# GpSimd's order around its row gathers, one pass for all rotary angles, and the query scaling on ScalarE

## The reference

```python
q = rmsnorm((x @ Wq.T).reshape(B, S, 32, 128), q_norm_w)      # B = 32, S = 32, x is 32 x 32 x 512
k = rmsnorm((x @ Wk.T).reshape(B, S, 8, 128), k_norm_w)
v = (x @ Wv.T).reshape(B, S, 8, 128)
pos = cache_seqlens[:, None] + arange(S)
q, k = rope(q, pos), rope(k, pos)                             # cos and sin of pos / 10000^(2i/128)
k_all = concat([k_cache[block_table], k]); v_all = concat([v_cache[block_table], v])   # 512 + 32 keys
probs = softmax(where(valid, q @ k_all / sqrt(128), -1e30))   # 4 query heads share a key head
x = x + (probs @ v_all) @ Wo.T
```

## Time and profile before

| | |
|---|---|
| median of 3 runs | 1675.08 us (1672.77 to 1676.43) |
| the profiled execution | 1681.27 us, its span 1679.5 us |
| PE busy, share of the span | 1383.3 us, 82% |
| DVE | 998.1 us, 59% |
| POOL | 983.9 us, 59% |
| ACT | 769.5 us, 46% |
| mean granted clock of TensorE | 0.92 |
| DMA | 207.04 MB, 123 GB/s over the span |

### The profile page before, as it was taken

The page is one execution under the profiler, slowest core; times in us unless marked ns, Lnnn a source line. Parts: engine busy times, 40 slices in busy tenths (PEclk is TensorE's granted clock), DMA queues, the critical chain, the costliest instruction groups (busy, mean ns, idle before and its releaser), DMA issues. The chain is left out here.

```text
span 1679.5 us, 29186 instructions
## 1 busy us (share of the span) xinstructions
PE 1383.3 (82%) x8896; PEld 1255.8 (75%) x8896; DVE 998.1 (59%) x2478; ACT 769.5 (46%) x1965; POOL 983.9 (59%) x1264
## 2 busy tenths in 40 slices
PE   3678888897878898887887888898787888888899
PEld 2577778786768787776777777787677887777887
DVE  5755656565565665556655555566666565555664
ACT  3444454444454444445444454444445444445541
POOL 5556666656665556666646666556666555665610
PEclk8799999998899999889998999999989998889999
DMA  5453343345343434435335343333535343433431
GB/s 188 146 156 121 96 129 101 107 126 163 115 148 108 130 107 132 125 91 157 125 115 170 96 125 100 107 115 126 172 116 156 105 118 120 125 96 124 120 103 51
DMA packets 73244, 207.04 MB, mean 123 GB/s; under 512 B 12177, under 2 KB 12465, under 8 KB 73009
## 3 DMA queue, kind: packets, MB, share of 16 engines
q0 software_dynamic: 40960, 134.25, 26.6%
q1 hardware_dynamic: 31392, 69.53, 13.1%
q10 hardware_dynamic: 816, 2.29, 0.4%
HBM read 195.77 MB, written 12.36 MB: 124 GB/s over the span
## 5 line engine op out<-in xcount | busy, mean ns | idle before, releaser
L1062 POOL DMA_INDIRECT kv_rows<-in_kv,step_idx x512 | 510.4, 997 | 188.6 <-issue 132.7
L815 DVE CUSTOM_DVE_ANT_0 soft<-SX,mask 128x544 f32<-128x544 f32 x256 | 185.0, 723 | 342.9 <-PE SX L181 342.4
L397 PE MATMUL KT<-ident,kv_rows 128*128 128x128 f32 x1024 | 177.7, 302 | 241.6 <-DMA kv_rows<-in_kv,step_idx 234.8
L397 PEld LDWEIGHTS KT<-ident,kv_rows 128*128 128x128 f32 x1024 | 128.8, 153 | 259.1 <-issue 236.2
L637 ACT ACTIVATE soft<-soft,min_all 128x544 f32<-128x544 f32 x256 | 191.9, 749 | 260.2 <-DVE min_all L815 257.3
L633 ACT ACTIVATE pT<-PT 128x640 f32<-128x640 f32 x256 | 178.8, 698 | 279.5 <-PE PT L438 279.4
L449 PEld LDWEIGHTS O<-pT,kv_rows 128*128 128x128 f32 x2048 | 283.4, 206 | 17.1 <-ACT pT L633 3.0
L449 PE MATMUL O<-pT,kv_rows 128*128 128x128 f32 x2048 | 290.2, 288 | 1.4 <-ACT pT L633 1.4
L181 PE MATMUL SX<-kT,qT_hi 128*128 128x288 f32 (+1 forms) x1024 | 255.2, 341 | 14.4 <-DVE qT_lo L861 11.7
L615 ACT ACTIVATE kT<-KT 128x512 fp32r<-128x512 f32 x256 | 151.3, 591 | 230.7 <-PE KT L397 230.7
L181 PEld LDWEIGHTS SX<-kT,qT_hi 128*128 128x128 f32 x1024 | 185.3, 219 | 18.7 <-DVE qT_lo L861 13.1
(11 more groups left out here) (207 smaller groups left out, 2604.4 us busy)
## 6 DMA issues: line engine op xcount, KB each, us to landing
mask<-mask_rows SPq DMA_DIRECT2D x64, 272.0 KB, 3.3
stage<-in_wqkv SPq DMA_DIRECT2D x22, 512.0 KB, 5.2
x_raw<-in_xT SPq DMA_DIRECT2D x32, 256.0 KB, 3.9
kv_rows<-in_kv,step_idx POOLq DMA_INDIRECT x512, 3.7
stage<-in_wo SPq DMA_DIRECT2D x16, 512.0 KB, 3.8
y_tile<-y_running SPq DMA_DIRECT2D x32, 256.0 KB, 3.3
y_running<-y_tile SPq DMA_DIRECT2D x31, 256.0 KB, 4.1
out<-kv_rows SPq DMA_DIRECT2D x8, 256.0 KB, 2.0
```

The costliest lines, as they stand in the source:

```text
L397: tr = nc.tensor.transpose(KT[:, c * P:(c + 1) * P], kv_rows[:, b, c, h * D:(h + 1) * D], ident[:, :])
L815: V.tensor_tensor_reduce(scores[:, p % 2, :], SX[:, SX_AT:SX_AT + KEYS], mask[:, b, :], 1.0, BIG, ALU.add, ALU.min, min_all[:, p:p + 1]).t ...
L1062: G.indirect_dma_start(kv_rows[:, b, c, :], None, kv[:, :], bass.IndirectOffsetOnAxis(ap=step_idx[:, b * LC + c:b * LC + c + 1], axis=0)). ...
```

## The change

It has five parts.

- **GpSimd's order.** The gather of b = 3 comes first in a step, with its indices taken in one copy with the others in the step before. Then `rotate_sum` for k = 0, the indices of all four batch elements, gather(0), `rotate_sum` for k = 1, gather(1), `rotate_sum` for k = 2, gather(2), the table.
- **What left GpSimd.** `keep_v` is now four ScalarE copies of 32 rows each (the rest of `v_own` is zeroed once). The mean square is a small VectorE operation (`mean_square`, at pairs 1, 3 and 5). The scaling of the rotated queries by `rstd` is four ScalarE copies of 128x128 with a scale operand (`scale_q`, at pairs 3 and 5, after `exponent`). The keys are still scaled on GpSimd.
- **TensorE.** In pair 7 the first 6 matmuls of `project_out` stand ahead of `score` instead of behind it.
- **The angles.** All 8 tiles in one pass, one range reduction for sine; the cosine is Sin(pi/2 - |angle|), by a scale and a bias of the activation. The tables of the first step are made on VectorE, the row indices on GpSimd.
- **The start.** The blocks of weights are split into high and low parts by halves, the activation table for Exp is loaded before the first block is taken, the mask row is made earlier, and the first pairs' work is put in another order.

The core of the diff (`idx_ready`, `v_zero`, `row_in` and the like are semaphores; the start's new order is left out):

```diff
+            def scale_q(i, h):
+                nth = i * NBLK + h + 2
+                act.wait_ge(sm["sum_ready"], nth)
+                act.wait_ge(sm["pow_ready"], nth)
+                act.wait_ge(sm["q_turned"], i * GK + h)
+                act.nop(nofuse=True)
+                for r in range(REP):
+                    cols = slice(r * D, (r + 1) * D)
+                    scaled = nc.scalar.activation(q_rot[:, cols], rope_u[:, cols], ACT.Copy, scale=rstd[:, r:r + 1])
+                scaled.then_inc(sm["rot_ready"], 1)
+
+            def keep_v(i):
+                act.wait_ge(sm["raw_ready"], i * NBLK + 1)
+                act.wait_ge(sm["pv_done"], CREDIT + i * PAIRS)
+                act.nop(nofuse=True)
+                for b in range(ROWS):
+                    rows = slice(b * SEQ, (b + 1) * SEQ)
+                    kept = nc.scalar.activation(v_own[rows, b, :], v_next[rows, :], ACT.Copy)
+                kept.then_inc(sm["v_own_ready"], 1)
...
+                    if not last and p in (3, 5):
+                        scale_q(i + 1, p // 4)
                     if not last and p == 6:
                         take_qT(i + 1, 1)
...
+                    if not last and p == PAIRS - 1:
+                        keep_v(i + 1)
...
+            def mean_square(i, k):
+                n = GK if k == 0 else REP
+                dve.wait_ge(sm["sq_ready"], i * NBLK + k + 1)
+                V.tensor_scalar(meansq[:, k, 0:n], sumsq[:, k, 0:n], 1.0 / D, EPS, ALU.mult, ALU.add
+                                ).then_inc(sm["ms_ready"], 1)
...
+                    if p == PAIRS - 1:
+                        project_out(i, 0, (0, REP // 2), g * HALVES + WO_FIRST + 2)
                     if p + 2 < PAIRS:
                         score(i, p + 2)
...
-                    if p == PAIRS - 1:
-                        project_out(i, 0, (0, REP // 2), g * HALVES + WO_FIRST + 2)
...
                 G.tensor_tensor(rope_u[:, 0:w], rope_u[:, 0:w], rope_v[:, 0:w], ALU.add).then_inc(sm["sum_ready"], 1)
+                pool.wait_ge(sm["ms_ready"], nth)
+                pool.wait_ge(sm["rot_ready"], nth - 1)
+                G.tensor_tensor(rstd[:, 0:n], meansq[:, k, 0:n], minus_half[:, 0:n], ALU.pow).then_inc(sm["pow_ready"], 1)
                 pool.wait_ge(sm["sum_ready"], nth)
                 pool.wait_ge(sm["pow_ready"], nth)
-                if k == 0:
-                    pool.wait_ge(sm["kT_new_done"], i)
-                    dst = k_rot[:, :]
-                else:
-                    pool.wait_ge(sm["q_turned"], i * GK + k - 1)
-                    dst = q_rot[:, :]
+                if k > 0:
+                    return
+                pool.wait_ge(sm["kT_new_done"], i)
...
-                for k in range(2):
-                    make_rstd(i + 1, k)
-                    rotate_sum(i + 1, k)
-                for row in range(ROWS - 1):
+                b = ROWS - 1
+                pool.wait_ge(sm["pv_done"], CREDIT + i * PAIRS)
+                pool.nop(nofuse=True)
+                gather(b, 0, LC)
+                if last:
+                    return
+                rotate_sum(i + 1, 0)
...
+                for row in range(ROWS):
                     pool.wait_ge(kv_in[row], (i + 1) * 16 * LC)
-                take_indices(tn, 0, ROWS - 1, 2 * i + 3)
+                take_indices(tn, i + 2)
                 next_values(0)
-                make_rstd(i + 1, 2)
+                rotate_sum(i + 1, 1)
+                next_values(1)
                 rotate_sum(i + 1, 2)
+                next_values(2)
                 if not (final and fixed and t == TILES - 2):
                     make_table(i + 2, (t + 2) % TILES if fixed else t + 2)
-                next_values(1)
-                next_values(2)
```

More of the change, by code:

```diff
@@ L121, in program @@
         minus_half = sb("minus_half", [P, REP])
+        half_pi = sb("half_pi", [P, 1])
         row_i = sb("row_i", [BATCH, 1], I32)
@@ L240, in next_tile, with table_parts @@
             return (g + 1, 0) if isinstance(t, int) and t == TILES - 1 else (g, t + 1)
+        def table_parts(t):
+            c, s = ((a[:, t, :] if isinstance(t, int) else a[:, bass.ds(t, 1), :].rearrange("p a n -> p (a n)"))
+                    for a in (cos, sin))
+            for z in range(2):
+                for f in range(2):
+                    cols = slice(f * 64, (f + 1) * 64)
+                    other = slice((1 - f) * 64, (2 - f) * 64)
+                    yield table[:, 2 * z, cols], c, norm_w[:, z, cols]
+                    yield table[:, 2 * z + 1, cols], s, norm_w[:, z, other]
         block = ctx.enter_context(nc.Block())
@@ L381, in proj @@
                         pe.wait_ge(sm["x_ready"], i + 1)
+                    if k == NBLK - 1 and new_keys_first:
+                        pe.wait_ge(sm["kT_new_ready"], i + 1)
                     pe.wait_ge(sm["raw_ready"], i * NBLK + k)
@@ new lines, in _ @@
+            pool.wait_ge(sm["idx_ready"], 1)
+            for j in range(PPC):
+                q = slice(j * PSIZE, (j + 1) * PSIZE)
+                G.tensor_scalar(row_base[q, :], pages_f[q, :].rearrange("p (a j) -> p a j", j=PPC)[:, :, j],
+                                float(PSIZE), in_page[q, 0:1], ALU.mult, ALU.add).then_inc(sm["idx_ready"], 1)
+            pool.wait_ge(sm["idx_ready"], 1 + PPC)
+            take_indices(0, 1)
+            gather(0, 0, LC)
+            G.memset(v_own[:, :, :], 0.0).then_inc(sm["v_zero"], 1)
```

235 lines of the change are left out of this document (97 added, 138 removed).

## The result

The changed kernel took 1500.52 us (median of 4 runs, 1498.61 to 1503.25), against 1673.92 us (4 runs) for the kernel before: a ratio of 0.8969, 95% interval 0.8942 to 0.8997. So it is 10.3% faster. The forecast was 1480 us, 20.5 us or 1.4% too low, and the range held the time. In the experiments all chips were not alike: the kernel before took between 1669 and 1688 us on them. The changed kernel ran on two chips, 1500.5 and 1501.1 us, while the kernel before took 1674 and 1688 on them, so its ratio differs between them (0.8969 and 0.8887). The times of variants of the changed kernel are therefore set against 1500.5 to 1501.1, and differences of a few us are read only between kernels of one chip. Two executions of variants ran slow (1524.8 us with the scaling back on GpSimd, 1852.1 us with the scaling in pair 4), and the times given for these two are medians of the others.

A forecast was written before the change was run, and what follows sets the result against it. TensorE was taken as the bound, waiting 234.8 us for gathered rows behind GpSimd's work. From 1675.1 us, -339 (waits and lower clock) + 155 (given back) - 11.5 (start) gave 1480 us, range 1395 to 1595.

The forecast's parts named there:

- the sum: Whole kernel: 339 us saved in the steps, 155 given back, 11.5 saved at the start, together -195.5 us.
- The start: Ahead of the steps: angles in one early pass and earlier first products bring -11.5 us, bounds 6 and 16.
- The keys: TensorE's waits for gathered rows at pairs 5 and 7 go, 234 us, with the gather starting at 13.6 us.
- The given-back 5.0 us: Pairs 4 to 7, per step: later scaled queries, `pT` and projection cost 1.1, 0.5, 1.9 and 1.5 us.
- The lower clock, 105 us: Pairs 5 and 7: TensorE's lower clock after key waits costs 3.4 us a step over 31 steps, and goes.
- The 16 us that the range allowed for those: Tiles 6, 7 and 0: weight splitting, until now partly under the key wait, may cost about 1 us each.
- my walk through the new order: Ahead of the steps: first product 2 us earlier, queries' transposes 3 to 4, first pair at 48 us.
- Edits at nothing: In the steps: `keep_v`'s ScalarE copies, VectorE's mean squares and GpSimd's lost work were charged no time of their own.
- The clock rival: Pairs 4 to 7: four gaps in 20 us lower the clock, 3.4 us a step stay, 1585 us; chance 0.18.
- The keys were not late: Pair 5: rival with keys 4 to 5 us later, about 2.5 us of waiting left, 1617 us; chance 0.10.
- the 1.06 us at which the gain would have been gone: ScalarE's eight scaling copies a step: slower rival, no gain at 1.06 us each, 1735 us at 1.3; chance 0.05.
- Less given back: Pairs 4 to 7: rival with only ScalarE's load left, about 1.7 us a step, 1378 or halfway 1430; chance 0.20.

The follow-up runs named there:

- the order alone: Kernel before with only GpSimd's step order changed, gathers of b = 0 and 1 ahead of the next block's work: 1459.32 us, on another chip 1472.23.
- the scaling in pair 4: Changed kernel with the first query block's four ScalarE scaling copies moved from pair 3 to behind pair 4's `pT` and `kT` copies: 1468.58 us.
- the projection behind the scores: Changed kernel with the first six output projection matmuls of pair 7 back behind `score`: 1485.90 us.
- the copies run twice: Changed kernel with four more 128x128 scaling copies on ScalarE ahead of the real four in both blocks, into an unread tile: 1576.32 us.
- with both causes taken away: Changed kernel with the first block's scaling copies behind pair 4's copies and pair 7's first six projection matmuls behind `score`: 1471.92 us.
- The angles alone: Kernel before with only the one-pass angles for all eight tiles and the cosine from the sine's argument: 1681.77 us, ratio 0.9963.

## Why the prediction was right, and by how much its steps missed

**Where the 20.5 us are.** From the first pair's start to that of the last step, the 31 steps took 59.48 to 1603.86 before and take 54.36 to 1422.84 now: 1544.4 and 1368.5 us, 175.9 saved where the sum has 339 - 155 = 184. Some 5 of these 8 us are the sum's own: it counts 234 us of waits for all steps, while 31 steps like the one it reads, with 7.37 us of them, hold 228.5. The start gives 5.1 us where it has 11.5. The last step and the end are as before (75.6 us in both). Together 181.1 against 195.5, 14.4 short. The other 6.2 us are the choice to go by the median of before instead of its profiled execution. The changed kernel's profiled execution (span 1498.4) lies at its median, and against 1681.27 us the forecast would have been 1485.8.

**The keys: right.** The gather was put at 13.6 us after the step's start and is at 13.3; 234 us of waits were to go and 228.8 went. The order alone shows that GpSimd's order does all of it. What left GpSimd was not needed for this, and the prediction, which credited the order and let the rest "only make room", was right on that too.

**The given-back 5.0 us: right in sum and nearly so pair by pair.** The step was forecast at 42.8 and is 42.9. Pairs 4 to 7 were put at 5.8, 3.6, 5.2 and 9.9 us (full-clock pairs of 4.7, 3.1, 3.3 and 8.4, plus 1.1, 0.5, 1.9 and 1.5) and take 5.69, 4.02, 5.60 and 9.28. The named mechanisms are there: ScalarE's wait of 2.73 us at pair 3 (forecast 2.9), the copies' 1.28 (1.2), the power's end at 20.6 (20.9), pair 5's wait for the earlier output (0.41 us, `oT_lo` ready at 26.4, forecast 26.6), the second mean square, power and copies (29.3, 30.4 and 31.8, forecast 28.7, 29.8 and 31.1), and `project_out`'s wait for `oT_lo` in pair 7. The first is shown by the scaling in pair 4, the last by the projection behind the scores, and the load of the copies by the copies run twice. The exact split is luck in part: with both causes taken away, the waits turn up elsewhere. Two things the walk did not have. TensorE's second largest wait, 24.0 us, is for `qT_lo`, which it did not name. And pair 6 follows an operation that is held up on VectorE. The division of the probabilities at 26.5 us takes 1.48 us instead of 0.50 beside GpSimd's sum, in all 31 steps, and `kT`'s low part, the mean square, the power and the copies come behind it. At most 1.0 us a step hangs on this. With the scaling in pair 4 the division is rarely caught, but the second block's mean square is (0.87 us instead of 0.15). No run keeps VectorE clear of GpSimd's sum, and none gives the mean square back to GpSimd, so what either costs is not shown.

**The lower clock, 105 us: right in size, but not all of it clock.** Without their waits pairs 5 and 7 took 9.23 - 4.35 = 4.88 and 13.01 - 3.02 = 9.99 us before, and in the order alone, with the same work on TensorE, they take 3.07 and 8.42. That is 1.8 and 1.6 us, as forecast (to 3.1 and 8.4). TensorE's busy time fell by less, 72.4 us there (to 1310.9) and 52.5 in the changed kernel (1383.3 to 1330.8). Short waits also lengthen what counts as busy. From the transposed keys at 485.96 to the scores at 487.35 are 1.39 us, with 0.73 of idle time. Undisturbed, in pair 4, the same starts are 0.35 apart (475.56 and 475.91), so that wait cost 1.04 at a granted clock of 1.00. A part of the 1.8 and 1.6 is of this kind too. The lengths of the steps hold both, and only their sum is measured. By the step that it reads, the prediction saves 5.8 us a step (48.5 to 42.7). The 20 regular steps save 5.6 each, which makes the other 3 of the 8 us by which the steps fell short, and the 11 with work on weights 5.8. The 16 us that the range allowed for those were not needed.

**The start: the term that was mis-sized.** It was put at -11.5 with bounds of 6 and 16, and 5.1 lies outside them. The step that failed is "my walk through the new order puts the first pair at 48". The angles alone do bring the first pair to 48.49. The rest of the new start loses 5.9 us of it. In the changed kernel TensorE waits there:

```profile
35.16 1.11 PE L423 MATMUL MISC<-ident,q_rot 128*128 128x128 f32 x4 [4.26 <-ACT q_rot L639]
...
50.31 1.12 PE L423 MATMUL PROJ<-ident,q_rot 128*128 128x128 f32 x4 [3.14 <-ACT q_rot L639]
```

The walk had the queries' transposes 3 to 4 us earlier. They come 1.4 us later than before at the first block (35.16 against 33.74) and 4.7 later at the second (50.31 against 45.61). With the scaling back on GpSimd the second block's transposes come at 47.03 and the first pair starts at 51.09, both 3.3 us earlier than in the changed kernel. So the scaling holds some 3.3 of the 5.9 us, and the rest was not separated. The figure is rough: with the projection behind the scores, an edit that leaves the start as it is, the first pair starts at 52.33, and five traces with the changed kernel's start have it between 52.33 and 55.12.

**Edits at nothing: right where tested.** `keep_v` makes no difference on either engine. The mean squares were not tested alone. That of the first block takes 1.70 us instead of 0.15, but ends with the sum that the power waits for anyway (476.17 and 476.14), so it costs nothing. That of the second block is in the chain of pair 6, where the prediction had put it.

**The rivals.** The clock rival is refuted for the regular steps (1.00 in all 20, with gaps of up to 0.73 us), and of the other 11 six read 0.95 or 0.96, while the rival needed a lower clock in every step. But the copies run twice show that it was near: behind waits of 0.44, 0.73 and 1.36 us the clock was 0.50. The row that the prediction set against this rival was weak. From 1604 to 1632 TensorE has one gap of 0.79 us and one of 0.26, not several near 1 us. The keys were not late. A copy takes a third of the 1.06 us at which the gain would have been gone. "Less given back" is what the order alone achieved, with 41.2 us a step, by leaving the scaling and the projection where they were. The prediction saw that moving it cost 155 us against the floor, but took the part as given and never priced its opposite. The queries would have been ready at the same time on GpSimd.

## What to carry to other kernels

When a wait goes away because work was put in another order, try the order alone before anything is moved to another engine; here the one edit of order gave more than the steps' whole gain (222 us of the 31 steps against 176), and the rest of the change took back 40 us (1501.1 against 1460.8 with the same pass for the angles). Before work moves to an engine in order to relieve another, ask when the result will be ready on either: if the last producer stays where it was, the move brings nothing, and a wait for it blocks whatever is queued behind it. A late low part shows up in whichever matmul comes next, so measure two such repairs together, on one chip with each alone, before you add their gains. And compare the starts of the same rows in the same step: where chips differ by 13 us, a median 15 us lower does not say which part gave it.

## What the runs showed of the hardware

Small VectorE operations took many times their usual length beside a GpSimd product or sum of two tiles. In the changed kernel the mean square of 128x4 took 1.70 us where it took 0.15 at other places, and the division of the probabilities 1.48 instead of 0.50. GpSimd's 1.28 us sums of 128x512 stand at 474.86 and 483.07. The mean square ends with the first (476.17 and 476.14), the division 0.31 us behind the second:

```profile
474.47 1.70 DVE L851 TENSOR_SCALAR meansq<-sumsq 128x4 f32<-128x4 f32 x1
476.79 0.50 DVE L870 TENSOR_SCALAR soft<-soft,rden 128x544 f32<-128x544 f32 x1
...
483.18 1.48 DVE L870 TENSOR_SCALAR soft<-soft,rden 128x544 f32<-128x544 f32 x1
485.83 0.15 DVE L851 TENSOR_SCALAR meansq<-sumsq 128x4 f32<-128x4 f32 x1
```

The same shows for the rounding of the input (`x_hi`, 128x512), which stands beside `keep_v`. It takes 0.43 us on average in the changed kernel and 1.42 with `keep_v` on GpSimd.

The Trainium skill, GPSIMD Engine Reference, section 1. Specifications, says that GpSimd shares its interfaces to the on-chip memory with VectorE, and names VectorE's two-input operations and its faster modes as the ones that contend. The rows agree in that VectorE is held up beside GpSimd, by 0.7 to 1.6 us for an operation caught so. The ones caught here read one tile each, and no row shows whether they ran in a faster mode.

What it costs depends on what waits for the operation that is caught. The longer roundings cost nothing: the kernel with them was no slower. The first block's mean square cost nothing either. The division in pair 5 and, in the order alone on one of the chips, the copy of the new keys stand ahead of what TensorE waits for.

The second point is the clock. In a step with gaps of 0.4 to 0.7 us it read 1.00. Behind a stretch with TensorE busy for 1.64 of 4.00 us it read 0.50. Where between them it gives way these runs don't show.
